# One tap of the depthwise convolution from TensorE to VectorE, and one from VectorE to GpSimd

## The reference

```
t  = einsum('bchw,oc->bohw', x, w_in)            # 384 -> 384 channels
tf = rfft2(t by 8x8 patches) * fft_filter         # then irfft2 back to pixels
t  = irfft2(tf)
t  = conv(t, w_dw, 3x3, padding SAME, groups=384) # one 3x3 filter per channel
x1, x2 = t[:, :192], t[:, 192:]
g  = gelu(x1) * x2
x  = x + einsum('bchw,oc->bohw', g, w_out)
```

## Time and profile before

| | |
|---|---|
| median of 3 runs | 3602.86 us (3592.69 to 3609.84) |
| profiled execution | 3610.5 us, span of its instructions 3608.4 us |
| PE busy | 3351.8 us (93%) |
| DVE busy | 3006.7 us (83%) |
| POOL busy | 2046.6 us (57%) |
| ACT busy | 1709.3 us (47%) |
| mean granted clock of TensorE | 0.976 of full speed |

### The profile page before, as it was taken

One profiled execution on the slowest core, in us unless ns is written; L12 is line 12 of the kernel. 1 busy time (PEld: TensorE's weight loads), 2 busy tenths in 40 slices (PEclk: granted clock), 3 DMA queues, 4 the chain that ended last, 5 costly groups with the idle time before them and its releaser, 6 DMA issues. The chain is left out here.

```text
span 3608.4 us, 50305 instructions
## 1 busy us (share of the span) xinstructions
PE 3351.8 (93%) x17430; PEld 2901.3 (80%) x17430; DVE 3006.7 (83%) x5252; ACT 1709.3 (47%) x3138; POOL 2046.6 (57%) x1343
## 2 busy tenths in 40 slices
PE   5999989999899999999999999999999999999998
PEld 4987779777797777977789777897778967799776
DVE  7977988779897698987989869788798887988877
ACT  1433844338443474434744357342574426644265
POOL 2554755547556474564755647456474565654555
PEclk9999999999999999999999999999999999999999
DMA  6214332143312333123321233312332133321422
GB/s 220 71 45 158 115 105 72 61 149 108 119 63 67 135 120 108 62 79 123 132 97 62 97 115 124 104 62 100 120 123 97 53 123 105 123 90 60 140 97 96
DMA packets 185339, 369.89 MB, mean 103 GB/s; under 512 B 7770, under 2 KB 8834, under 8 KB 184834
## 3 DMA queue, kind: packets, MB, share of 16 engines
q1 hardware_dynamic: 185090, 366.68, 29.7%
HBM read 265.99 MB, written 100.66 MB: 102 GB/s over the span
## 5 line engine op out<-in xcount | busy, mean ns | idle before, releaser
L1124 PE MATMUL bank<-w_hi,x_hi 128*128 128x384 f32 x2304 | 803.1, 349 | 19.3 <-ACT vt L575 10.0
L444 POOL TENSOR_TENSOR t<-t 128x768 f32<-128x768 f32 x256 | 534.8, 2089 | 468.8 <-DVE t L829 464.8
L1125 PE MATMUL bank<-w_lo,x_hi 128*128 128x384 f32 x2304 | 778.8, 338 | 0.0
L993 DVE SCALAR_TENSOR_TENSOR bank<-big,wdw,bank 128x512 f32<-128x512 f32 x1072 | 750.5, 747 | 22.4 <-PE bank L1305 19.4
L437 POOL TENSOR_TENSOR x_lo<-xa,x_hi 128x512 fp32r<-128x512 f32 x360 | 459.0, 1290 | 526.0 <-ACT x_hi L564 526.0
L509 POOL TENSOR_TENSOR prod<-prod 128x512 f32<-128x512 f32 x320 | 412.2, 1288 | 256.5 <-ACT prod L667 238.1
L1129 PE MATMUL bank<-w_hi,x_lo 128*128 128x384 f32 x2304 | 531.5, 339 | 0.5 <-POOL x_lo L437 0.5
L569 ACT ACTIVATE t<-t 128x384 f32<-128x384 f32 x256 | 134.7, 526 | 767.5 <-POOL t L444 749.9
L1124 PEld LDWEIGHTS bank<-w_hi,x_hi 128*128 128x128 f32 x2304 | 434.1, 188 | 26.4 <-issue 25.8
L1125 PEld LDWEIGHTS bank<-w_lo,x_hi 128*128 128x128 f32 x2304 | 434.9, 189 | 2.3 <-issue 1.7
L1129 PEld LDWEIGHTS bank<-w_hi,x_lo 128*128 128x128 f32 x2304 | 413.4, 188 | 1.4 <-POOL x_lo L437 1.4
(11 more groups left out here) (131 smaller groups left out, 7042.9 us busy)
## 6 DMA issues: line engine op xcount, KB each, us to landing
xr<-x SPq DMA_DIRECT2D x128, 768.0 KB, 4.8
xa<-x SPq DMA_DIRECT2D x64, 768.0 KB, 6.3
x_scratch<-xr SPq DMA_DIRECT2D x64, 768.0 KB, 3.3
xa<-x_scratch SPq DMA_DIRECT2D x64, 768.0 KB, 6.0
xr<-x_scratch SPq DMA_DIRECT2D x64, 768.0 KB, 4.9
out<-xr SPq DMA_DIRECT2D x64, 768.0 KB, 3.3
big<-x SPq DMA_DIRECT2D x8, 768.0 KB, 10.2
w_raw<-wqkv_t SPq DMA_DIRECT2D x1, 1728.0 KB, 7.0
```

Of the source, the lines that this page charges most:

```text
L444: nc.gpsimd.tensor_tensor(a, a, b[:, :, ::-1, :], ALU.add).then_inc(s_add, 1)
L993: nc.vector.scalar_tensor_tensor(dst, src, wdw[:, k, q:q + 1], so_far, ALU.mult, ALU.add)\
L1124: nc.tensor.matmul(dst, hi(k), whi(k), start=(k == 0), stop=False)
L1125: nc.tensor.matmul(dst, hi(k), wlo(k), start=False, stop=False)
```

## The change

Three numbers change, and two orders that depend on them.

- PE no longer makes tap (0, 1) in steps 1 to 7. DVE makes it instead, as the first instruction of that sum: a tensor_scalar from `big` to the bank. Step 8, in which PE makes six taps of each block, keeps its twelve.
- POOL sums one tap more of block 2: ACT makes a product for tap 6 as well, POOL adds it, and DVE begins with (7, 2) instead of (6, 2). Tap 6 needs the row below, so its product and its addition stand one step later than the other six, at the head of ACT's and POOL's work in the step.
- DVE begins the late taps with (6, 0) and (7, 0), and takes (7, 2) third. On ACT the first `copy_t` of the step stands ahead of the three products of the next chunk, behind the product of tap 6. Product 0 now waits for (7, 2).

The diff, cut to its core:

```
-PE_TAPS, PE_BLOCKS = 1, 2
+PE_TAPS, PE_BLOCKS = (1, 0), 2
-POOL_TAPS = 6
+POOL_TAPS = 7
-EARLY = [(1, 0), (2, 0), (1, 1), (3, 0), (2, 1), (4, 0), (3, 1), (5, 0), (4, 1), (5, 1)]
-LATE = [(6, 2), (6, 0), (7, 2), (7, 0), (8, 2), (8, 0), (6, 1), (7, 1), (8, 1)]
+EARLY = [(1, 0), (0, 1), (2, 0), (1, 1), (3, 0), (2, 1), (4, 0), (3, 1), (5, 0), (4, 1), (5, 1)]
+LATE = [(6, 0), (7, 0), (7, 2), (8, 0), (8, 2), (6, 1), (7, 1), (8, 1)]
...
                 def part_c(c, h, edge, par):            # POOL
+                    if c >= 2:
+                        add_product(c - 2, 6)
                     if within(edge, 0, NCH, -1):
                         for q in range(1, 3):
                             add_product(c - 1, q)
...
                         if not first:                   # ACT, product
-                            act.wait_ge(s_dw, dw_count(i, c - 1, (6, 2)))
+                            act.wait_ge(s_dw, dw_count(i, c - 1, (7, 2)))
...
+                    if gated:                           # ACT, part_c
+                        if c < NCH + 1:
+                            act.wait_ge(s_img, (i * 8 + c - 1) * 4 + 6)
+                        product(c - 2, 6)
+                    if tile:
+                        copy_t(T, 0)
                     if conv:
                         for q in range(3):
                             product(c - 1, q, edge == 1)
-                    if tile:
-                        copy_t(T, 0)
...
-                    if q == (PE_TAPS, PE_TAPS, POOL_TAPS)[k] or (last and q == 6):
+                    if q == (*PE_TAPS, POOL_TAPS)[k] or (last and q == 6):
+                        if k == 1 and not last:         # DVE, tap
+                            dve.wait_ge(s_img, n * 4 + 6)
+                            dve.wait_ge(s_gate, n * 2 + 2)
+                            nc.vector.tensor_scalar(dst, src, wdw[:, k, q:q + 1], None, ALU.mult).then_inc(s_dw, 1)
+                            return
...
                         dve.wait_ge(s_img, T + 2)       # DVE, part_c
-                        tap(c - 2, 6, 2)
                         tap(c - 2, 6, 0)
+                        tap(c - 2, 7, 0)
+                    if gated:
                         tap(c - 2, 7, 2)
-                    if gated:
-                        tap(c - 2, 7, 0)
+                        tap(c - 2, 8, 0)
                         tap(c - 2, 8, 2)
-                        tap(c - 2, 8, 0)
                         tap(c - 2, 6, 1)
...
                     if conv:
                         tap(c - 1, 1, 0)
+                        tap(c - 1, 0, 1)
...
                     inverse_tile(T, 0)                  # PE, part_c
-                    if conv:
-                        taps(c - 1, 1)
                     t_tile(T + 3, m, par, 3)
```

More of the change, by code:

```diff
@@ L24 @@
 TAPS = 9
-PE_TAPS, PE_BLOCKS = 1, 2
+PE_TAPS, PE_BLOCKS = (1, 0), 2
 PE_LAST = (6, 6)
-POOL_TAPS = 6
+POOL_TAPS = 7
 NPROJ = NCH - 2
-EARLY = [(1, 0), (2, 0), (1, 1), (3, 0), (2, 1), (4, 0), (3, 1), (5, 0), (4, 1), (5, 1)]
-LATE = [(6, 2), (6, 0), (7, 2), (7, 0), (8, 2), (8, 0), (6, 1), (7, 1), (8, 1)]
+EARLY = [(1, 0), (0, 1), (2, 0), (1, 1), (3, 0), (2, 1), (4, 0), (3, 1), (5, 0), (4, 1), (5, 1)]
+LATE = [(6, 0), (7, 0), (7, 2), (8, 0), (8, 2), (6, 1), (7, 1), (8, 1)]
 NE = len(EARLY)
 ND = NE + len(LATE)
-LAST = [(6, 2), (6, 0), (7, 2), (7, 0), (8, 2), (8, 0), (6, 1), (7, 1), (8, 1)]
+LAST = LATE
 ND_IMAGE = (NCH - 1) * ND + len(LAST)
@@ L532, in part_c @@
                     if within(edge, 0, NCH, -1):
-                        for q in range(3, POOL_TAPS - 1):
+                        for q in range(3, 5):
                             add_product(c - 1, q)
@@ L537, in part_c @@
                     if within(edge, 0, NCH, -1):
-                        add_product(c - 1, POOL_TAPS - 1)
+                        add_product(c - 1, 5)
                     if within(edge, 0, NCH if i + 1 < images else NCH - 1):
@@ L983, in tap @@
                     so_far = dst
-                    if q == (PE_TAPS, PE_TAPS, POOL_TAPS)[k] or (last and q == 6):
+                    if q == (*PE_TAPS, POOL_TAPS)[k] or (last and q == 6):
[4 more added lines that the diff above has]
+                            return
                         if k < PE_BLOCKS:
-                            dve.wait_ge(s_ptap, n * PE_BLOCKS + (k + 1))
+                            dve.wait_ge(s_ptap, i * (NCH + 1) + c + k + 1)
                         else:
@@ L1030, in part_c @@
                     if last:
-                        for m, early in enumerate((LAST[0:2], LAST[2:4], LAST[4:6])):
+                        for m, early in enumerate((LAST[0:2], LAST[2:4], LAST[4:5])):
                             for q, k in early:
@@ L1037, in part_c @@
                             rope((i + 1) * NT, 0, 0)
-                        for q, k in LAST[6:]:
+                        for q, k in LAST[5:]:
                             tap(c - 2, q, k, last)
@@ L1294, in out_block, with taps @@
                     nc.tensor.matmul(dst, wout_lo[:, 1, cols], g_half[:, :], start=False, stop=True).then_inc(s_out, 1)
-                def taps(c, k, n_taps=PE_TAPS):
+                def taps(c, k, n_taps=PE_TAPS[0]):
                     n = i * 8 + c
```

## The result

| | before | after |
|---|---|---|
| median of the runs, us | 3603.9 (3592.7 to 3609.8, 4 runs) | 3652.3 (3642.4 to 3654.5, 4 runs) |
| profiled execution, us | 3610.5 | 3642.4 |

The ratio is 1.0124, with a 95% interval from 1.0108 to 1.0140. The changed kernel is slower by 1.2%, 48 us on the medians. The profiled execution of the changed kernel is the fastest of its four, so between the two profiles there are only 32 us.

A forecast was written before the change was run, and what follows sets the result against it. PE was taken as the bound, POOL's run close behind. Steps 1 and 2 -0.1, steps 3 to 6 +3.2, step 7 +0.5, steps 8 and 9 +0.65: 4.25 us an image, 34 on 3602.9, giving 3637; range 3600 to 3660.

The forecast's parts named there:

- The chain through ACT, POOL and DVE: Middle step, tap 6 to POOL's first addition: that starts at 5.63 us instead of 3.82, so `g_lo` ends at 14.63.
- Back to PE: Middle step from output block 0 at 14.68 us to the next second addition: 4.15 more, ending at 18.83.
- The middle step: Each of steps 3 to 6: 18.83 us against 18.04, 0.79 more, with bounds of +0.35 and +1.15.
- It is within 3% of being the bound itself: DVE in a middle step: its only idle gap is 0.52 us, right before the second addition of the residual.
- So PE sets the pace: Middle step before the change: PE is the limit, and POOL's run of 9.00 us has only 0.66 us of slack.
- the run is hidden, DVE is the bound: No-change rival: PE doesn't wait for `g_lo`, middle step 17.87 us (-0.17), time 3598 us; chance 0.13.
- My sum of DVE's work: DVE in a middle step: 17.37 us of work after the change, before waits, against 17.52 before it.
- Steps 1 and 2: Start of an image: step 1 gains PE's 0.86 us, step 2 loses it again; together -0.1.
- Step 7: Step in which PE waits for DVE: +0.5 us, from DVE's work up to its second `gb` plus waits.
- Steps 8 and 9: End of an image: POOL's run ends 3.2 us later, partly hidden by work falling into DVE's wait; +0.65 us.
- The clock: Rival: the granted clock falls in the middle steps, counted mostly as slower; chance 0.12.
- POOL's sum comes in time: Faster rival: sum with tap 6 ready when DVE reaches (7, 2), middle step -0.67 us, time 3574; chance 0.10.

The follow-up runs named there:

- e3_gate_first: Changed kernel with POOL's two subtractions for `g_half` and `g_lo` moved ahead of addition 4; 3648.2 us, ratio 1.0123.
- e2_dve_only: Kernel before the change, with only DVE making the first tap of block 1 and POOL keeping six taps; 3624.5 us, ratio 1.0057.
- e5_own_sums: Changed kernel with POOL's four product buffers used in turn, so the first three products don't wait for DVE's read of the sum; 3634.0 us, ratio 1.0079.
- e6_own_sums_copy_back: Changed kernel with product buffers used in turn and ACT's copy of the first projected tile behind the three products; 3672.6 us, ratio 1.0182.
- the last run: Changed kernel with buffers in turn, `g_lo` ahead of addition 4 up to step 7, DVE taps reordered, ACT rounding gated values before product 4; 3594.1 us, ratio 0.9973.

## Why the prediction was right, and where its working was wrong

*Direction and size.* Slower was forecast with +4.25 us an image; the stages show +5.16. The run's 3652 lies 15 us above the 3637 of the forecast, 7 of them from the stages. The other 8 lie between medians and profiles: the profiled execution of the changed kernel, 3642.4, had a granted clock of 0.979, the other three, 3652.0 to 3654.5, had 0.973 to 0.976.

*The chain through ACT, POOL and DVE.* Right to a few hundredths: the first addition at 5.63 as forecast, `g_lo` ended at 14.62 (14.63), DVE's wait of 0.46 (0.5), the sum's tap 0.76 (0.75), the tensor_scalar 0.747 with the next instruction 0.66 behind it, output block 0 at 14.68.

*Back to PE.* The tail from there was taken as 4.15 and measured 4.01. PE's own pace in it, without the small waits of the kernel before, is 0.55 faster than the 4.56 there. The middle step is +0.65 (18.69 against 18.04) instead of +0.79. But that PE's wait causes it was only half the truth: `e3_gate_first` takes 0.87 of the wait away and the step falls by 0.04.

*DVE's limit: the step that failed.* "It is within 3% of being the bound itself" read the 0.52 before the second addition as slack, and with "So PE sets the pace" DVE was left out of the sum. `e2_dve_only` shows that it is a hand-over and belongs to DVE's limit. So the rival "the run is hidden, DVE is the bound" would have been 17.67 + 0.48 + 0.51 = 18.66, not 17.87, and the step would have lost 0.6 by that way too. My sum of DVE's work, 17.37, was also 0.3 short: the first `gb` starts 0.79 behind the tap ahead of it and not 0.66, the narrow gate 0.08 later than before, and the rest is spread over waits of less than 0.1. The forecast of the middle step came out near because the two limits lie within 0.05 us of each other. That is luck: the working knew of only one of them.

*Steps 1 and 2.* -0.1 forecast, +0.45 measured; between images that have no half clock in these steps it is +0.24 (48.37 against 48.13). What it left out is the read of the sum in step 2: `e5_own_sums`, which frees the products from it, gives 0.68 of it back. And PE now waits 2.58 us for `gelu` before its tap in step 2. In the fourth image that wait fell together with 3.4 us at half clock (a granted clock of 0.70 and 0.79 in the two windows that share them, below), in the fifth it didn't; they differ by 0.6 us. The row of the fourth image, then the windows around it (us, busy us and counts of PE, PEld, DVE, ACT, POOL, granted clock, DMA share, GB/s):

```profile
1709.34 2.00 PE L1316 MATMUL bank<-big,tapdiag 128*128 128x512 f32 x2 [2.58 <-ACT gel L648]
```

```profile
1708.00:1711.40 3.40, 2.06 (x3) 1.06 (x4) 2.15 (x4) 3.35 (x7) 1.95 (x2) 0.70 0.00 0
1711.40:1714.80 3.40, 3.40 (x17) 2.79 (x17) 3.40 (x6) 2.80 (x5) 3.26 (x4) 0.79 0.00 0
1714.80:1718.20 3.40, 3.34 (x18) 2.27 (x16) 3.40 (x6) 3.16 (x6) 1.88 (x2) 1.00 0.00 0
```

*Step 7.* +0.5 forecast, +0.99 measured. DVE's three normalising tensor_scalars last 4.36 us and lasted 3.92 before, which is 0.44 of the missing 0.49. They last 3.40 in `e3_gate_first`, where POOL's order beside them is another; step 7 is 0.83 shorter there. The three rows, of the kernel before, of the changed kernel and of `e3_gate_first`:

```profile
2234.15 3.92 DVE L811 TENSOR_SCALAR xa<-xa,gmean,rstd 128x512 f32<-128x512 f32 x3
```

```profile
2249.50 4.36 DVE L817 TENSOR_SCALAR xa<-xa,gmean,rstd 128x512 f32<-128x512 f32 x3
```

```profile
2253.56 3.40 DVE L817 TENSOR_SCALAR xa<-xa,gmean,rstd 128x512 f32<-128x512 f32 x3
```

POOL works beside them in all three kernels; I had left out that its later start puts other instructions beside them. That they wait for POOL is argued from the tap of 1.77 us in `e6_own_sums_copy_back` and not shown by a run of its own.

*Steps 8 and 9.* +0.65 forecast, +1.16 measured. POOL's last addition ends 17.16 us after the last second addition instead of 13.77, 3.4 later (forecast 3.2); what hides in the wait was overrated. `e5_own_sums` gives 1.04 back.

*The rivals.* The clock, for whose fall the forecast has a chance of 0.12, did not fall in the middle steps: the 74.8 us from 2165.2, four of them, have a granted clock of 1.00, and so have those of the other seven images. Nor does half clock follow every long wait here: in the kernel before PE waits 2.3 us in step 7 of seven images, and half clock (0.50) followed in the fourth to the seventh of them but not in the first three. "POOL's sum comes in time" put the turning point at a first addition at 4.84. `e6_own_sums_copy_back` has it at 3.20 and is slower by 0.76 a step: that rival had reckoned with DVE's sum alone, and not with a tap of 1.77 us.

*Still open:* why the time at half clock in the unchanged parts differs between executions, from 89 to 145 us in the profiles, and so how much of the last run's gain is its order.

## What to carry to other kernels

Before an idle gap of the second-busiest engine is called slack, look at who it waits for and what that one had been waiting for: a ping-pong over one buffer belongs to the limit of both (0.52 of the 18.04 us here). Where two limits lie level, undoing one edit shows nothing, and only the pair does; one tap placed inside the hand-over was then worth 0.56 us a step, and DVE's tap in PE's place 0.16. Waits too short for the view to print add up to half a microsecond: compare the same stretch of instructions in two runs before a chain is called unbroken. And an earlier start on POOL can cost more than it gives: where its addition fell on DVE's tap with two inputs in SBUF, the tap took 1.77 us instead of 0.76, and the step 0.76 more (`e6_own_sums_copy_back` against the changed kernel).

## What the runs showed of the hardware

- DVE's tap with both inputs in SBUF took 0.76 us alone, in the changed kernel, and 1.77 when an addition of POOL had started 0.08 before it (`e6_own_sums_copy_back`).
- A tensor_scalar of DVE from SBUF to PSUM, 128x512 in fp32, took 0.747 us at the median, no less than a scalar_tensor_tensor that also reads the bank (0.747 too, both in the changed kernel).
- A wait of about 1.35 us of PE (1.29 to 1.65) in each of the steps 3 to 6 left the granted clock at 1.00 in all eight images. One of 2.58 in step 2 was followed by half clock (0.50) in the fourth image and not in the fifth, and one of 2.3 in step 7 of the kernel before in four images of seven.
